# Graph convolution on one Trainium2 core: visits in two pieces, steps of four chunks in straight code, and a histogram that begins with the sources as they lie

## The chip, the core and the metric

The kernel runs on one core of one Trainium2 chip. The time is in device microseconds (us) from the start of one execution to its end; a kernel's time is the median of its runs. TensorE (PE in the profile) does the matmuls, VectorE (DVE) and ScalarE (ACT) the elementwise work, GpSimd (POOL) issues the gathers, and SyncE (SP) passes signals on and issues some of the transfers. PSUM is the accumulator memory of TensorE: eight banks of 128 x 512 fp32, called `bank` in the kernel.

## The reference

Two graph convolutions over the same graph, with a layer norm and a leaky ReLU between them, and a residual with a layer norm behind them:

```python
def _cheb_norm(src, dst, n):
    deg = jax.ops.segment_sum(jnp.ones((src.shape[0],), jnp.float32), src, num_segments=n)
    dinv = jnp.where(deg > 0, jax.lax.rsqrt(jnp.maximum(deg, 1.0)), 0.0)
    return -dinv[src] * dinv[dst]
...
    def prop(h):
        return jax.ops.segment_sum(h[src] * norm[:, None], dst, num_segments=x.shape[0])
    out = x @ W0
    tx1 = prop(x)
    out = out + tx1 @ W1
    return out + b
...
    h = _cheb_conv(x, src, dst, norm, W1_0, W1_1, b1)
    h = _layer_norm(h, gamma, beta)
    h = jnp.where(h >= 0, h, NEG_SLOPE * h)
    out = _cheb_conv(h, src, dst, norm, W2_0, W2_1, b2)
    return out
...
    x = _layernorm(x + _L0_gnn_ref(...), axis=-1)
```

`x` is 6250 x 512 in fp32. There are 106250 edges (50000 random ones in both directions, and one loop per node), sorted by `dst`. Each weight is 512 x 512.

## The kernel before

The nodes lie in 49 tiles of 128 rows (`TILES`), and `acc` holds all of them in SBUF: first `x`, then the sums of a pass. The kernel has four stages.

**Histogram.** The degrees are counted by matmul. In each of 24 visits DVE makes two one-hot arrays for 36 chunks of 128 sources each (`lo_hot`, 128 values, and `hi_hot`, 49 values; L805 and L808), and PE adds 36 products of them in one bank (L668). In the same visit PE turns one tile of `x` (L655, `turn`), ACT moves it to `feat` and SP stores it as `feat_dram[0]`. ACT also takes the squares of a tile and counts, with `Sign` activations, how many edges lie below each tile's end. Before the first visit all edge numbers are turned by PE and copied by DVE. After the visits the other 25 tiles are turned.

**Table.** Each tile, scaled by the node's factor (`up`), is split into a high and a low fp16 half (ACT L507, DVE L878) and stored as a row of 1024 fp16 in `table[0]`. Behind that DVE makes the small tables that tell each step its tile, group and ring slot (`neg_tile`, `tile_i`, `group_i`, `slot_i`, `used_i`), and `walk_ready` lets PE, SP and DVE begin the first pass.

**Two passes** (`l` = 0 and 1), one for each convolution. POOL gathers the 832 chunks of 128 edges by indirect DMA, 256 KB each, from `table[l]` into a ring of 16 chunk slots in SBUF (L444). A group is 2 chunks, so there are 416 groups and 8 ring slots of one group; POOL waits on `ring_free` before each group. A step is one pair of a group and a tile, since a group's edges can lie across the end of a tile: 416 + 48 = 464 steps. In a step DVE makes one one-hot array per chunk from `dst_c` (L923), PE multiplies them with the chunk's two halves, 4 matmuls into one of 4 banks (L710), and DVE adds the bank, times `down`, to the tile's rows of `acc` (L947). SP waits until a group has landed (L389) and tells PE (`groups_ready`), and in the same loop waits until the steps that used the group of 4 earlier (`FREE_LAG`) are done and tells POOL that its slot is free (`ring_free`, L393). SP also copies each block of 16 index columns from `src_u` to `index` by DMA (L371).

**Visits.** Once the sums of a tile are complete, a visit makes its output. Steps run in blocks of 8. After each block but every seventh comes a visit, whose place is fixed; a comparison of `early` with the tile's number skips it there if a tile could be late, and then all that are left come at the end of the pass. All 49 come in their places with these inputs. A visit on PE is one row of work in program order: the product of `base_in` and `wB` (L727), the turn of the sums (`staged`, L655), in the first pass the turns of two earlier tiles' normalized and hidden rows (L655), and then the product of the turned sums and `wA` (L749), for which PE waits until ACT has moved the turned sums from PSUM to `feat` (L564, `turned_moved`). In the first pass the output is normalized (statistics on DVE, L991), turned, scaled, put through the leaky ReLU, turned back and stored as `table[1]`. In the second it is added to `x`, normalized and stored as `out`.

The loops over blocks, periods, gathers and SP's turns are hardware loops (`looped`), with a few turns written out at either end.

## Time and profile before

| | us |
|---|---|
| median of 3 runs | 3432.88 (3428.44 to 3451.5) |
| span of the profiled execution | 3370.7 |
| the profiled execution's own time outside its span, taken as median less span | 62.2 |
| PE busy | 2065.1 (61%) |
| DVE busy | 1544.4 (46%) |
| ACT busy | 505.3 (15%) |
| POOL busy | 1700.9 (50%) |
| data of DMAs | 559.98 MB, mean 166 GB/s |

The span runs from the first to the last instruction in the trace. The time holds the start and the end of the execution too. No engine is busy over all of the span, so what counts is who waits for whom. A name such as "L444 POOL" is line 444 of the kernel on GpSimd. PEld is TensorE's loading of weights, which overlaps its matmuls; SPq, ACTq and DVEq are an engine's sequencer, as opposed to its data path.

### The profile page before, as it was taken

To read this page: it belongs to the slowest core of one execution; us is meant where nothing else is said; L and a number is where in the kernel's file an instruction comes from. 1 tells how busy PE (TensorE), PEld (TensorE's weight loads), DVE (VectorE), ACT (ScalarE), POOL (GpSimd) and SP (SyncE) were. 2 spreads that over 40 slices of the span, in tenths; PEclk is the share of its full clock that TensorE was granted. 3 is DMA by queue.
4 is the path that set the end of the run, shared out by engine and by line. 5 is a ranking of instruction groups with operands and counts; after the bars stand their busy time and mean duration, and the time that the engine had idled before them with its cause. 6 is when DMAs were issued, how large, how long until landed. Compare 5 with 4: busy or idle time off the path is not lost.

```text
span 3370.7 us, 41016 instructions
## 1 busy us (share of the span) xinstructions
PE 2065.1 (61%) x7250; PEld 963.6 (29%) x7251; DVE 1544.4 (46%) x3507; ACT 505.3 (15%) x1030; POOL 1700.9 (50%) x1725
## 2 busy tenths in 40 slices
PE   6836576665665665665764656565565656555655
PEld 5712232222222322232331222222222222222222
DVE  6754444444444444544443444444444434444444
ACT  5920111111111211111230000000000000000000
POOL 0156554545555554655526545554545445554543
PEclk6558887887887878887876878787777777878778
DMA  6376565655555555655646555565555555555554
GB/s 215 133 259 181 150 174 155 173 159 160 164 167 168 159 165 157 181 159 167 182 132 200 166 158 171 166 177 155 167 159 164 155 158 165 161 165 162 159 159 122
DMA packets 215109, 559.98 MB, mean 166 GB/s; under 512 B 48100, under 2 KB 49760, under 8 KB 214948
## 3 DMA queue, kind: packets, MB, share of 16 engines
q0 software_dynamic: 133120, 436.31, 45.9%
q10 hardware_dynamic: 44676, 81.73, 7.2%
q1 hardware_dynamic: 37152, 40.21, 3.6%
q8 instruction: 50, 0.82, 0.1%
q14 instruction: 111, 0.91, 0.1%
HBM read 493.08 MB, written 64.18 MB: 165 GB/s over the span
## 4 chain that ended last, share of the span: by engine, by line
PE 30%; another core or an unknown queue 26%; issue 25%; DVE 8%; ACT 5%; DVEq 3%; ACTq 1%; DMA 1%; POOL 1%; SPq 0%; POOLq 0%
PE bank L749 16%; PE bank L710 10%; DVE acc L947 6%; PE bank L668 2%; ACT work L556 2%; ACT feat L564 1%; DVEq L923 1%; PE bank L727 1%; PE bank L655 1%; DVEq L947 1%; DVE onehot L923 1%; POOL ring L444 1%; ACT work L546 1%; ACTq L528 0%
## 5 line engine op out<-in xcount | busy, mean ns | idle before, releaser
L444 POOL DMA_INDIRECT ring<-table,index x1664 | 1672.6, 1005 | 1466.5 <-SPq L393 952.1
L947 DVE SCALAR_TENSOR_TENSOR acc<-bank,down,acc 128x512 f32 x928 | 696.9, 751 | 1219.6 <-PE bank L710 709.8
L710 PE MATMUL bank<-ring,onehot 128*128 x3712 | 920.3, 406 | 306.0 <-issue 148.1
L749 PE MATMUL bank<-wA,feat 128*128 128x512 f32 x784 | 547.6, 863 | 804.2 <-ACT feat L564 748.2
L923 DVE TENSOR_SCALAR onehot<-count_h,dst_c,neg_tile 128x128 f16<-128x128 f16 x1856 | 489.2, 329 | 490.1 <-issue 487.6
L710 PEld LDWEIGHTS bank<-ring,onehot 128*128 128x128 f16 x3712 | 380.6, 103 | 865.6 <-issue 515.3
L749 PEld LDWEIGHTS bank<-wA,feat 128*128 128x128 f32 x784 | 212.0, 285 | 1084.9 <-ACT feat L564 774.3
L727 PE MATMUL bank<-wB,base_in 128*128 128x512 f32 x784 | 353.6, 594 | 0.0
L546 ACT ACTIVATE work<-acc 128x512 f32 (+1 forms) x98 | 61.7, 630 | 1747.4 <-issue 1039.3
L727 PEld LDWEIGHTS bank<-wB,base_in 128*128 128x128 f32 x784 | 149.5, 191 | 155.8 <-issue 142.1
L564 ACT ACTIVATE feat<-bank 128x512 f32<-128x512 f32 x98 | 58.5, 597 | 845.4 <-remote 828.7
L655 PE MATMUL bank<-ident,work 128*128 128x128 f32 x588 | 88.3, 288 | 125.8 <-issue 99.7
L655 PEld LDWEIGHTS bank<-ident,work 128*128 128x128 f32 x588 | 67.1, 145 | 199.1 <-issue 181.7
L668 PE MATMUL bank<-ring 128*128 128x49 bf16 x864 | 85.2, 275 | 2.5 <-DVE ring L808 2.5
L668 PEld LDWEIGHTS bank<-ring 128*128 128x128 bf16 x864 | 83.6, 146 | 4.0 <-DVE ring L808 2.9
L598 ACT ACTIVATE feat<-bank,beta_c,gamma_c 128x128 f32<-128x128 f32 x196 | 73.8, 457 | 59.2 <-remote 39.5
L556 ACT ACTIVATE work<-acc,shift,rstd 128x512 f32 (+1 forms) x98 | 78.4, 800 | 6.6 <-DVE shift L960 3.0
L991 DVE BATCH_NORM_STATS2 stats<-acc 128x6 f32 (+1 forms) x98 | 67.5, 689 | 11.7 <-issue 9.5
L655 PE MATMUL bank<-ident,acc 128*128 128x128 f32 x196 | 52.4, 425 | 27.4 <-ACT feat L480 18.6
L805 DVE TENSOR_TENSOR ring<-work,base_in 128x4608 bf16<-128x4608 bf16 x24 | 61.4, 2559 | 14.4 <-PE bank L668 14.2
L421 POOL PARTITION_ALL_REDUCE row_max<-row_max x1 | 0.4, 382 | 126.0 <-DVE row_max L821 126.0
L613 ACT ACTIVATE acc<-bank 128x512 f32 (+1 forms) x49 | 29.4, 600 | 141.9 <-PE bank L749 132.7
(118 smaller groups left out, 689.6 us busy)
## 6 DMA issues: line engine op xcount, KB each, us to landing
ring<-table,index POOLq DMA_INDIRECT x1664
base_in<-feat ACTq DMA_DIRECT2D x98, 256.0 KB
feat<-feat SPq DMA_DIRECT2D x49, 256.0 KB, 2.9
table<-work SPq DMA_DIRECT2D x49, 256.0 KB, 3.1
feat<-feat ACTq DMA_DIRECT2D x49, 256.0 KB
table<-work ACTq DMA_DIRECT2D x49, 256.0 KB
feat<-in_x ACTq DMA_DIRECT2D x48, 256.0 KB
out<-work ACTq DMA_DIRECT2D x48, 256.0 KB
```

The source lines that it names most:

```text
L444: nc.gpsimd.indirect_dma_start(out=ring[:, at * ROW:(at + 1) * ROW], out_offset=None, in_=table[l], in_offset=bass.IndirectOffsetOnAxis(ap ...
L546: nc.scalar.activation(staged[it.slot % 2], tile_of(acc, it.n), ACT.Copy).then_inc(staged_ready, 1)
L556: nc.scalar.activation(normed[s], tile_of(acc, k.n), ACT.Identity, bias=shift[:, k.slot % 3:k.slot % 3 + 1], scale=rstd[:, k.slot % 3:k.sl ...
L564: nc.scalar.activation(feat[:, 2 + s, :], bank[TURN_BANK][:, :], ACT.Copy).then_inc(turned_moved, 1)
L598: last = nc.scalar.activation(feat[:, s, c * P:(c + 1) * P], bank[NORMED_BANK][:, c * P:(c + 1) * P], ACT.Identity, bias=beta_c[:, c:c + 1 ...
L655: last = nc.tensor.transpose(to[:, c * P:(c + 1) * P], src_tile[:, c * P:(c + 1) * P], ident[:, :])
L668: last = nc.tensor.matmul(bank[4][:, 0:TILES], lo_hot[it.slot % 2][:, :, j], hi_hot[it.slot % 2][:, :, j], start=it.least == 0 and j == 0, ...
L710: last = nc.tensor.matmul(bank[u % SUM_BANKS][:, :], onehot[:, u, j, :], ring[:, bass.ds(at, D)], start=j + half == 0, stop=j + half == GROUP)
L727: nc.tensor.matmul(to[:, :], base_in[:, tile_slot, c * P:(c + 1) * P], wB[:, c * D:(c + 1) * D], start=c == 0, stop=False)
L749: last = nc.tensor.matmul(to[:, :], feat[:, 2 + tile_slot, c * P:(c + 1) * P], wA[:, c * D:(c + 1) * D], start=False, stop=c == KB - 1)
L923: last = nc.vector.tensor_scalar(onehot[:, slot, j, :], count_h[:, :], col(dst_c, group * GROUP + j), col(neg_tile, n), ALU.subtract, ALU. ...
L947: nc.vector.scalar_tensor_tensor(tile_of(acc, tile[u]), bank[u % SUM_BANKS][:, :], col(down[:, l, :], tile[u]), tile_of(acc, tile[u]), ALU ...
```

## The change

Group and step: a group is 4 chunks, a pass has 208 groups and 208 + 48 = 256 steps of 8 matmuls. The ring keeps its 16 chunk slots, now 4 groups, and `FREE_LAG` is 2. DVE makes the one-hot arrays of two steps in one instruction, from `rel` (for each step and chunk, the edges' places relative to the step's tile) and a row of counts in PSUM; it adds a step's bank to `acc` without a factor, and the factor `down` comes in where the sums are turned, by a product with the diagonal matrix `diag`.

Visits: a visit has two pieces on PE, `begin` (the turn of the tile before, the product with `wB`, the turn of the sums) and `complete` (the product with `wA` and the turn of the hidden rows), two steps apart (`PRODUCT_LATER`). ACT's move of the turned sums lies between them. Visits come 5.2 steps apart. DVE's part comes 1 and 3 steps after `begin`.

Loops: the passes are written out, with no hardware loops on any engine. The gathers take their indices from a whole table in SBUF, so SP's index DMAs are gone, and they have no bounds check.

Histogram: 26 visits of 32 chunks, with 4 sources of a node value side by side in the one-hot arrays. It begins with the sources of the first 128 groups as they lie, one group to a partition, since a count doesn't depend on where an edge lies; the turn into columns for the gathers comes behind the first visit. Counts 0 to 255 and the identity are made on DVE, and the count of groups below each tile's end is made by DVE and two small matmuls in place of ACT's `Sign`. From the third visit on PE turns two tiles of `x` in each. The tables for the steps are made behind the table stage (`tables`, `relative`), and the lateness of visits, the bias parts and the second pass's factors behind the first one-hot arrays.

```diff
     LAST_ROWS = N - (TILES - 1) * P
     BOUNDS = TILES - 1
-    GROUP = 2
-    GROUPS = -(-E // (GROUP * P))
+    GROUP = 4
...
     CHUNKS = GROUPS * GROUP
     STEPS = GROUPS + BOUNDS
-    UNROLL = 8
-    STEP_BLOCKS = STEPS // UNROLL
-    GATHER_BLOCKS = GROUPS // UNROLL
-    RING = UNROLL
-    FREE_LAG = 4
...
+    RING = 16 // GROUP
+    FREE_LAG = RING // 2
...
     SUM_BANKS = 4
-    HIST_VISITS = BOUNDS // 2
-    HIST = 36
...
+    HIST = 32
+    RUN = 4
+    HIST_VISITS = CHUNKS // HIST
...
-    LAG_STATS, LAG_NORMAL, LAG_HIDDEN, LAG_LEAKY, LAG_BACK, LAG_LOW = 1, 2, 3, 4, 5, 6
...
+    SPACING = STEPS * 256 // TILES
+    FIRST_PLACE = -(-STEPS // TILES) + 8 // GROUP
+    PRODUCT_LATER, LEAKY_LATER, STATS_LATER = 2, 1, 3
...
-                def pass_on(it, l=l):
...
-                    for k in range(UNROLL):
-
-                        sp.wait_ge(ring_landed[k], 16 * GROUP * (GATHER_BLOCKS * l + it.n + 1))
-                        sp.sem_inc(groups_ready, 1)
-                        if k >= first:
-
-                            sp.wait_ge(steps_done, used[k - first] + STEPS * l)
-                            sp.sem_inc(ring_free, 1)
...
+                for g in range(GROUPS):
+                    k = g % RING
...
+                    sp.wait_ge(ring_landed[k], 16 * GROUP * ((GROUPS * l + g) // RING + 1))
+                    sp.sem_inc(groups_ready[l], 1)
+                    if g >= FREE_LAG:
+
+                        sp.wait_ge(steps_done[l], used[g - FREE_LAG - first])
+                        sp.sem_inc(ring_free, 1)
...
-                def gathers(it, l=l):
-                    pool.wait_ge(index_in[it.slot], 16 * (GATHER_BLOCKS // 2 * l + it.turn + 1))
-                    pool.sem_inc(gathers_begun, 1)
...
-                        wait(pool, ring_free, GROUPS * l + it.n * UNROLL + k - RING + 1)
...
-                        for j in range(GROUP):
...
-                            nc.gpsimd.indirect_dma_start(
-                                out=ring[:, at * ROW:(at + 1) * ROW], out_offset=None, in_=table[l],
-                                in_offset=bass.IndirectOffsetOnAxis(ap=index[:, it.slot, at:at + 1], axis=0),
-                                bounds_check=bound, oob_is_err=False).then_inc(ring_landed[k], 16)
-
-                straight(gathers, 0, 2, 2)
-                looped(pool, gathers, 2, GATHER_BLOCKS, 2)
...
+                for g in range(GROUPS):
...
+                    wait(pool, ring_free, GROUPS * l + g - RING + 1)
+                    for j in range(GROUP):
+                        at = k * GROUP + j
+                        c = index_col(g * GROUP + j)
+                        nc.gpsimd.indirect_dma_start(
+                            out=ring[:, at * ROW:(at + 1) * ROW], out_offset=None, in_=table[l],
+                            in_offset=bass.IndirectOffsetOnAxis(ap=index[:, c:c + 1].bitcast(U32), axis=0)
+                        ).then_inc(ring_landed[k], 16)
...
+            for v in range(HIST_VISITS):
+                pe.wait_ge(hot_ready, v + 1)
+                for j in range(HIST):
+                    last = nc.tensor.matmul(bank[4][:, 0:TILES], lo_hot[v % 2][:, j // RUN, :, j % RUN],
+                                            hi_hot[v % 2][:, j // RUN, :, j % RUN],
+                                            start=v == 0 and j == 0, stop=v == HIST_VISITS - 1 and j == HIST - 1,
+                                            skip_group_check=True)
+                last.then_inc(hist_done, 1)
...
+                for k in range(max(2 * (v - TURN_LATER), 0), max(2 * (v - TURN_LATER) + 2, 0)):
+                    turn_x(k)
...
+            def step(l, n, need, slot_at):
+                g = STEPS * l + n
+                for j in range(GROUP):
...
+                            if n % BLOCK == 0:
+                                pe.wait_ge(onehots_ready, g // BLOCK + 1)
+                            if n == 0:
+                                wait(pe, sums_added, g - SUM_BANKS + 1)
+                            pe.wait_ge(groups_ready[l], need & NEED)
+                        if j == GROUP - 1 and half == 1 and n + 1 < STEPS:
...
+                            wait(pe, sums_added, g + 1 - SUM_BANKS + 1)
+                        last = nc.tensor.matmul(bank[n % SUM_BANKS][:, :], hot,
+                                                ring[:, bass.ds(slot_at + (2 * j + half) * D, D)],
+                                                start=j + half == 0, stop=j + half == GROUP)
+                last.then_inc(steps_done[l], 1)
...
+            def turn_sums(l, v, steps):
+
+                pe.wait_ge(sums_added, STEPS * l + steps)
...
+                for c in range(KB):
+                    last = nc.tensor.matmul(bank[TURN_BANK][:, c * P:(c + 1) * P],
+                                            acc[:, bass.ds(v * D + c * P, P)], diag[:, v % 2, :],
+                                            start=True, stop=True)
+                last.then_inc(sums_turned, 1)
+
+            def sums_product(l, v):
+
+                pe.wait_ge(sums_moved, TILES * l + v + 1)
+                dense(out_bank(numbered(v)), sums_t[v % 2], wA, False).then_inc(out_done, 1)
...
+            def begin(l, v, steps):
+                if l == 0 and v > 0:
+                    turn_normed(v)
+                base_product(l, v)
+                turn_sums(l, v, steps)
+
+            def complete(l, v):
+                sums_product(l, v)
+                if l == 0 and v > 0:
+                    turn_hidden(v)
...
-                        pe.wait_ge(staged_ready, TILES * l + it.n + 1)
-                        wait(pe, turned_moved, TILES * l + it.n)
-                        turn(staged[tile_slot], bank[TURN_BANK], sums_turned)
...
-                        nc.tensor.matmul(to[:, :], ones_b[0:BIAS_PARTS, :], bias_parts[:, l * D:(l + 1) * D],
-                                         start=False, stop=False)
-                        pe.wait_ge(turned_moved, TILES * l + it.n + 1)
-                        for c in range(KB):
-                            last = nc.tensor.matmul(to[:, :], feat[:, 2 + tile_slot, c * P:(c + 1) * P],
-                                                    wA[:, c * D:(c + 1) * D], start=False, stop=c == KB - 1)
-                        last.then_inc(out_done, 1)
...
-                walk(pe, early, steps, visit)
...
+                for n in range(STEPS):
...
+                    step(l, n, entry[2 * (n % LOADED)], entry[2 * (n % LOADED) + 1])
+                    for v in range(BOUNDS):
+                        if place(v) == n + 1:
+                            with pe.If(early > v):
+                                begin(l, v, n + 1)
+                        if due(v, PRODUCT_LATER) == n + 1:
+                            with pe.If(early > v):
+                                complete(l, v)
...
+            dve.wait_ge(s_src[0], 16)
+            low_high(0, P * GROUP, edge_in[0][:, 0, :])
...
+            def sources(v):
+                wait(dve, hist_done, v - 1)
...
+                nc.vector.tensor_tensor(lo_hot[v % 2], lo_want.unsqueeze(1).to_broadcast([P, runs, P, RUN]),
+                                        columns(src_lo, P), ALU.is_equal)
+                nc.vector.tensor_tensor(hi_hot[v % 2], hi_want.unsqueeze(1).to_broadcast([P, runs, TILES, RUN]),
+                                        columns(src_hi, TILES), ALU.is_equal).then_inc(hot_ready, 1)
...
+            for k in range(TILES):
+                low_rows(k)
+            tables()
+            relative()
             dve.sem_inc(walk_ready, 1)
...
+            def hots(l, b):
...
+                nc.vector.tensor_tensor(onehot[:, b % 2, :, :], count_p.unsqueeze(1).to_broadcast([P, HOTS, P]),
+                                        rel[:, b * HOTS:(b + 1) * HOTS].unsqueeze(2).to_broadcast([P, HOTS, P]),
+                                        ALU.is_equal).then_inc(onehots_ready, 1)
...
-                def hot(n, tile, slot):
...
-                    for j in range(GROUP):
-                        last = nc.vector.tensor_scalar(onehot[:, slot, j, :], count_h[:, :],
-                                                       col(dst_c, group * GROUP + j), col(neg_tile, n),
-                                                       ALU.subtract, ALU.is_equal)
-                    last.then_inc(onehots_ready, 1)
...
-                def steps(b, least, l=l):
...
-                        dve.wait_ge(steps_done, STEPS * l + n + 1)
-
-                        wait(dve, sums_added, STEPS * l + n)
-                        nc.vector.scalar_tensor_tensor(tile_of(acc, tile[u]), bank[u % SUM_BANKS][:, :],
-                                                       col(down[:, l, :], tile[u]), tile_of(acc, tile[u]),
-                                                       ALU.mult, ALU.add).then_inc(sums_added, 1)
...
+                    dve.wait_ge(steps_done[l], n + 1)
+                    wait(dve, sums_added, g)
+                    nc.vector.tensor_tensor(acc_at, acc_at, bank[n % SUM_BANKS][:, :], ALU.add).then_inc(sums_added, 1)
+                    if n % BLOCK == BLOCK - 1:
+                        hots(l, n // BLOCK + 2)
```

TensorE in the first pass, a visit between two blocks of steps, before:

```order
L287 COMPARE_AND_BRANCH
L727 MATMUL bank<-wB,base_in 128x512 x4
L655 MATMUL bank<-ident,work 128x128 x8
L655 MATMUL bank<-ident,feat 128x128 x4
L745 MATMUL bank<-bias_parts,ones_b 128x512
L749 MATMUL bank<-wA,feat 128x512 x4
L287 UNCONDITIONAL_BRANCH
L698 TENSOR_LOAD group_i
L698 TENSOR_LOAD slot_i
```

and now, the first piece, with the step behind it:

```order
L795 COMPARE_AND_BRANCH
L638 MATMUL bank<-ident,work 128x128 x4
L708 MATMUL bank<-wB,base_in 128x512 x4
L741 MATMUL bank<-bias_parts,ones_b 128x512
L752 MATMUL bank<-diag,acc 128x128 x4
L795 UNCONDITIONAL_BRANCH
L697 REGISTER_ALU
L701 ISA
L701 MATMUL bank<-ring,onehot 128x512
```

and two steps on, the second piece:

```order
L701 ISA
L701 MATMUL bank<-ring,onehot 128x512
L798 COMPARE_AND_BRANCH
L708 MATMUL bank<-wA,work 128x512 x4
L638 MATMUL bank<-ident,feat 128x128 x4
L798 UNCONDITIONAL_BRANCH
```

The turn of the sums, now a product with `diag`, and the product with `wA`, which stood in one row, have two steps of 8 matmuls (L701) between them. The turn of the normalized rows has moved ahead of the product with `wB`, and that of the hidden rows behind the product with `wA`.

VectorE in a pass, where it goes over from the adds of one block to the one-hot arrays of the next, before:

```order
L947 ISA
L947 SCALAR_TENSOR_TENSOR acc<-bank,down,acc 128x512
L947 ISA
L947 SCALAR_TENSOR_TENSOR acc<-bank,down,acc 128x512
L929 TENSOR_LOAD tile_i
L923 ISA
L923 TENSOR_SCALAR onehot<-count_h,dst_c,neg_tile 128x128
L923 ISA
L923 TENSOR_SCALAR onehot<-count_h,dst_c,neg_tile 128x128
```

and now, at any place between visits:

```order
L1029 TENSOR_TENSOR onehot<-bank,rel 128x1024
L1128 TENSOR_LOAD tile_i
L1134 ISA
L1134 TENSOR_TENSOR acc<-acc,bank 128x512
L1134 ISA
L1134 TENSOR_TENSOR acc<-acc,bank 128x512
L1029 TENSOR_TENSOR onehot<-bank,rel 128x1024
L1134 ISA
L1134 TENSOR_TENSOR acc<-acc,bank 128x512
```

What came in blocks of 16 one-hot arrays and 8 adds is now one wide one-hot instruction behind every second add, and 2 adds stand between two one-hot instructions.

## Rows read from the trace of the kernel before

**Rows 1.** The page: span, then costliest groups (xcount, busy us, mean ns, idle time before).

```profile
span 3370.7 us, 41016 instructions
...
L444 POOL DMA_INDIRECT ring<-table,index x1664 | 1672.6, 1005 | 1466.5 <-SPq L393 952.1
...
L947 DVE SCALAR_TENSOR_TENSOR acc<-bank,down,acc 128x512 f32 x928 | 696.9, 751 | 1219.6 <-PE bank L710 709.8
...
L710 PE MATMUL bank<-ring,onehot 128*128 x3712 | 920.3, 406 | 306.0 <-issue 148.1
...
L923 DVE TENSOR_SCALAR onehot<-count_h,dst_c,neg_tile 128x128 f16<-128x128 f16 x1856 | 489.2, 329 | 490.1 <-issue 487.6
```

**Rows 2.** Waits, whole span: engine and line, releaser, us in total, times, longest us.

```profile
POOL ring L444 <- SPq L393: 952.1, 182, 11.6
...
ACT feat L564 <- remote: 828.7, 91, 13.3
...
PE bank L749 <- ACT feat L564: 748.2, 83, 13.0
```

**Rows 3.** Timeline, second pass, one visit with gathers under way (start us, us, engine, line).

```profile
2636.36 1.04 PE L655 MATMUL bank<-ident,work 128*128 128x128 f32 x4 [2.64 <-issue]
...
2642.09 1.00 POOL L444 DMA_INDIRECT ring<-table,index  x1 [0.30 <-issue]
...
2645.26 0.60 ACT L564 ACTIVATE feat<-bank 128x512 f32<-128x512 f32 x1 [8.32 <-remote]
...
2645.91 5.78 PE L749 MATMUL bank<-wA,feat 128*128 128x512 f32 x8 [7.97 <-ACT feat L564]
...
2651.53 7.07 PE L710 MATMUL bank<-ring,onehot 128*128 x32
...
2653.40 1.00 POOL L444 DMA_INDIRECT ring<-table,index  x1 [10.31 <-SPq L393]
```

**Rows 4.** Timeline, end of the first pass: a visit after the last gather.

```profile
1725.68 1.00 POOL L444 DMA_INDIRECT ring<-table,index  x1 [0.30 <-issue]
...
1744.95 0.60 ACT L564 ACTIVATE feat<-bank 128x512 f32<-128x512 f32 x1 [0.72 <-PE bank L655]
...
1774.87 1.00 POOL L444 DMA_INDIRECT ring<-table,index  x1 [48.19 <-issue]
```

**Rows 5.** Busy time by stretch: us and, in brackets, instructions of each engine, granted clock, DMA.

```profile
1786.00:1798.00 12.00, 7.10 (x22) 2.15 (x20) 3.00 (x4) 0.00 (x0) 9.26 (x10) 0.78 0.71 198
...
1802.00:1814.00 12.00, 0.00 (x0) 0.00 (x0) 0.75 (x1) 0.00 (x0) 9.00 (x9) 0.50 0.70 200
...
201.30:1712.00 1510.70, 948.80 (x3149) 423.53 (x3150) 689.00 (x1646) 238.24 (x494) 828.44 (x821) 0.81 0.58 167
...
1775.00:3335.00 1560.00, 925.85 (x2824) 390.55 (x2824) 668.31 (x1601) 99.25 (x187) 832.71 (x832) 0.78 0.57 165
```

**Rows 6.** Timeline, the stage ahead of the first gather.

```profile
134.72 1.05 PE L655 MATMUL bank<-ident,acc 128*128 128x128 f32 x4
...
135.56 3.55 PE L668 MATMUL bank<-ring 128*128 128x49 bf16 x36
...
139.15 0.21 DVE L817 TENSOR_SCALAR deg<-bank 128x49 f32<-128x49 f32 x1 [4.75 <-PE bank L668]
...
46.53 2.56 DVE L805 TENSOR_TENSOR ring<-work,base_in 128x4608 bf16<-128x4608 bf16 x1 [0.67 <-PE bank L668]
...
201.28 1.69 POOL L444 DMA_INDIRECT ring<-table,index  x1 [6.16 <-issue]
...
L878 DVE SCALAR_TENSOR_TENSOR work<-acc,up,work 128x512 f16<-128x512 f16 (+1 forms) x49 | 34.4, 745 | 11.2 <-ACT work L507 11.2
```

**Rows 7.** Timeline, last gather and last store.

```profile
3333.24 1.00 POOL L444 DMA_INDIRECT ring<-table,index  x1 [0.30 <-issue]
...
3363.73 0.27 ACTq L587 DMA_DIRECT2D out<-work  x1
```

**Rows 8.** The page: a queue that fetches instructions (packets, MB, share of 16 engines).

```profile
q14 instruction: 111, 0.91, 0.1%
```

1165 lines of the change are left out of this document (634 added, 531 removed).

## Prediction

> **What bounds the kernel now.** I read the page's costliest groups first, then the waits, then the timeline of one cycle of the ring, then the same work with no gathers under way, then busy time by stretch.
>
> The groups say that no engine is full: POOL issues 1664 gathers at 1.005 us each and is idle as long again, 952.1 us of it waiting for SP to free a ring slot [rows 1, 2]. The second large pair of waits is one chain: ACT waits 828.7 us for something marked "remote" before it moves the turned sums (L564), and PE waits 748.2 us for that move before the product with wA (L749) [rows 2].
>
> The timeline shows how the two belong together. In the second pass PE ends the turn of a tile's sums at 2637.40 (2636.36 + 1.04), and ACT, whose only need is that turn's signal, starts at 2645.26, after 8.32 us of waiting. What happened between is that POOL started the last of 16 gathers at 2642.09; about 3.2 us after it ACT moves. Then comes the product, 5.78 us, and then 32 matmuls of steps in 7.07 us, 0.221 each, and with their first steps the next gather at 2653.40, after 10.31 us idle [rows 3]. At the end of the first pass, where the last gather started at 1725.68 and the next one comes only 48.19 us later, the same L564 follows PE's turn in 0.72 us [rows 4]. So the signal is late while gathers stream and prompt when they don't. Two stretches of the same pass say it of all engines: at the same DMA rate (198 and 200 GB/s) and 10 and 9 gathers, PE ran 22 matmuls in one and none in the other, and DVE 4 instructions and 1 [rows 5]. Bandwidth is therefore not the bound. The kernel runs in cycles: POOL fills 16 slots in 16 x 1.305 = 20.9 us (1.005 and the gap of 0.30) and in the later part of it the signals of the other engines stop arriving; the ring fills, POOL stops, the signals come through, PE works off its queue, and slots come free. 1664 / 16 = 104 such cycles would be the least; 182 waits add to 952.1 us, 9.15 us per 16 gathers.
>
> **Ahead of the first gather.** Before, the histogram ends at 139.15; the 36 matmuls of a visit take 3.55 us, 98.6 ns each, and one turn of x 1.05 [rows 6]. Now PE is the likely pace: 832 matmuls x 0.0986 = 82.0, 49 turns x 1.05 = 51.5, and some 8 for the small turns and products, 142 us. It can start once the first sources have landed and been split, which I put at 12 us, an estimate (one load and four small DVE operations stand ahead, in place of all loads, turns and copies of the edges), so it ends at about 154, 15 later. From 139.15 to the first gather at 201.28 it was 62.1 us: 49 DVE operations of the table stage at 0.745 are 36.5, their waiting for ACT 11.2, and 14.4 are left for the factor ahead and the small tables behind [rows 6]. Now the moves of x no longer trail into the table stage (2 of waiting in place of 11.2), and the largest row norm is taken during the histogram (9.1 in place of 14.4): 154 + 36.5 + 2 + 9.1 = 201.6, **0 us**. Bounds: DVE's wide one-hot array took 2.56 and, by its width, the narrow one 1.0 [rows 6], 3.6 for 36 chunks; 32 chunks at that rate are 3.2 and hide under PE's 5.4 per visit; if the layout with 4 sources side by side ran at half the rate, 12 + 26 x 6.4 = 178 would be the end, +24. If PE ran at double clock there, 15 could be gained.
>
> **Steps.** PE's matmuls rise from 3712 to 4096, since each of the 96 pairs that cross a tile's end costs 8 matmuls instead of 4: 384 x 0.221 to 384 x 0.406 = 85 to 156 us of PE [rows 1, 3]. They aren't all on the path: PE is busy 925.85 of the 1560 us of a pass [rows 5]. They lie mostly in the time when PE works off its queue, though, so I carry them in the cost of a cycle below. DVE's 1856 one-hot instructions (489.2 us) become 256 wide ones, and 928 adds (696.9) become 512; at 0.751 an add that is 384 us [rows 1]. What a wide one takes no row shows; between 8 x 0.1 (no fixed part) and 8 x 0.329 = 2.6 us it is at most 674 us in all. DVE was not waited for, so I count **0**, with its order as a bound: an add behind a wide one-hot can be 2.6 us late, and PE has 4 banks of slack against that.
>
> **The visit.** The wait of PE for ACT's move gets two steps in front of the product. What it hides depends on the size of the wait: 748.2 / 98 = 7.6 us a visit, of which 16 matmuls at 0.256 (nearer to 0.221 than to the mean of 0.406, since they run off a queue) cover 4.1 if their chunks have landed. 3.5 remain. By PE's own account a visit with its steps then takes 20.6 busy (19.1 before, by 1874.65 us in both passes over 98, plus 3.9 matmuls and the slower turn), 3.5 of waiting and the 4.6 of other idle time that it has now: 28.7, against 31.3 now (3070.7 over 98). That is -258 over the passes.
>
> **The pauses**, from POOL's side. The slots and their bytes are the same, so are the cycles, 104. What follows a filled ring is now: landing and release 2.2 (from the last gather's end at 2643.09 to ACT's start, [rows 3]), then, where PE had stopped within the steps, one step of 8 matmuls and its signals, 2.6: 4.8 us. Where it had stopped at a product, 2.2 + 0.6 for the move + 5.78 for the product + a step of 2.6 = 11.2. Before, the second kind was the rule, since 98 visits' waits take most of 104 cycles: 83 waits of PE at L749 [rows 2]. With two steps between the pieces I take one cycle in four: 0.75 x 4.8 + 0.25 x 11.2 = 6.4. 104 x 6.4 = 666 against 952: **-286**. The two accounts agree to 10%, and I take this one, since POOL's chain has no gaps in it.
>
> **Between the passes and behind the last gather.** The first pass's last gather starts at 1725.68 and the second's first 48.19 us after its end [rows 4]; in it lie steps, and then visits' pieces with lags of up to 6 visits that have to be drained one by one (LAG_LOW). Now the lags are one tile, so of some five drained rows two are left: 31, **-18**. From the last gather at 3333.24 to the last store at 3363.73 and the end at 3370.7 it is 37.5 [rows 7]; with its product and normalization alone behind the last step, 25, **-12**.
>
> **Loops, bounds checks and index DMAs.** POOL's cadence of 1.305 was the same in every row, at loop ends too; without the bounds check it could fall, by at most the 0.30 of the gap: 0 to -0.3 x 1664 = -499, but only where the ring has a slot free. As the ring empties at PE's pace I take **0**. The Trainium skill, page "Runtime: NRT & Kernel Launch", section "Instruction fetch mechanics", says that a taken branch breaks the sequential prefetch and costs a fetch by DMA, and that unrolled code is preferred for that. By that rule the late signals could be late instructions, fetched behind the gathers' packets. The larger of the two queues that fetch instructions moved 111 packets in the whole execution, 0.1% of the span [rows 8], for some 100 turns of hardware loops: the rows neither exclude it nor speak for it. It is the rival "full flow" below.
>
> **The sum**, against the profiled execution: 3370.7 + 0 - 286 - 18 - 12 = 3054.7; with the 62.2 outside the span, which is the median's remainder, **3117 us**.
>
> **Rivals.**
>
> *Full flow.* The late signals come of the loops or of the sheer number of instructions and signals, and straight code with half of them doesn't have it. For it: streaming alone doesn't stop the signals, for they still come through 11 to 23 us after the second pass's first gather [rows 4, 5]. Against it: in the cycle shown ACT moves as soon as the last gather is out [rows 3], and a late instruction of ACT would not end just there. It would give up to 3054.7 + 286 - 952.1 = 2389 of span, 2451 with the rest, and PE would then be nearly full (20.6 us busy of the 22.2 that 1664 / 98 = 17 gathers at 1.305 take), which I price at 100: about 2550.
>
> *Little gained.* The signals stay as late, and PE now stops at the product in half of the cycles, since two steps ahead of it also need chunks that haven't been passed on: 0.5 x 4.8 + 0.5 x 11.2 = 8.0, x 104 = 832, -120 in place of -286: 3283. For it: landed chunks are announced by SP, whose signals are late as well.
>
> *Slower.* Freed slots come in fours of chunks, and with a lag of 2 groups POOL waits, in each cycle, for a whole step and a piece of a visit: 11.2 every time, 1165 us, +213 against now, so 3433 + 213 - 30 = 3616. It decides from a pause of 9.4 us on (952.1 and the 30 of the other terms, over 104). For it: a group of 4 needs 4 landings and 8 matmuls before it frees anything, at 0.406 each where the clock is low [rows 1]. Against it: two groups, 8 chunks, can always be on the way meanwhile.
>
> *Late visits* (a tile that misses its place puts all others behind the pass) would cost over 98 x 5 us; by the graph's own counts each tile has its last group two steps or more ahead of its place. 1 in 100.
>
> **How the numbers follow.** Forecast with its own range 2950 to 3260: 0.52. Full flow 0.22, little gained 0.15, slower 0.09, late visits 0.01, no effect at all 0.01. About 1% is what a measurement of this kernel can tell from no change. Within 1% (3399 to 3467) falls part of the way from little gained to slower: 0.06; above it 0.09; faster 0.85. The range goes from the full flow's 2540 to 3400, which leaves out the slower cases and the lowest part of full flow.
>
> **What would show it.** In the new profile: POOL's wait for SP at the gathers, 666 us in about 104 waits, each near 5 or 11; ACT's wait for PE's turn still marked "remote" and 7 us or more; PE's wait at the product with wA halved; the first gather near 201; between the passes 31. If POOL's wait is below 300 us and ACT's move follows PE's turn in under 1 us with gathers under way, full flow was right and my reading of the signals' cause was wrong. If the first gather comes after 215, the one-hot layout is slow. The forecast fails most likely through its one argued number, the share of cycles in which PE stops at a product.

## The result, and the profile after

The changed kernel takes **2681.27 us** (2671.0 to 2690.22, 4 runs) against 3436.52 for the kernel before: a ratio of 0.780, 95% interval 0.7775 to 0.7834. I had forecast 3117 with a range of 2540 to 3400, so the time lies in the range, but the gain is 755 us and not 316. The profiled execution has a span of 2688.4 us and a time of its own of 2690.22.

The page, as in [rows 1]: the span, the gathers, the steps' matmuls, DVE's adds, its one-hot arrays, and the product with wA, which L708 shares with that of wB.

```profile
span 2688.4 us, 28747 instructions
...
L397 POOL DMA_INDIRECT ring<-table,index x1664 | 1575.8, 947 | 940.6 <-issue 467.0
L701 PE MATMUL bank<-ring,onehot 128*128 x4096 | 1012.7, 403 | 177.1 <-SPq L361 87.1
L1134 DVE TENSOR_TENSOR acc<-acc,bank 128x512 f32 x512 | 351.3, 686 | 1622.7 <-remote 881.3
...
L708 PE MATMUL bank<-wA,work 128*128 128x512 f32 x784 | 429.0, 698 | 174.3 <-ACT work L496 148.5
...
L1029 DVE TENSOR_TENSOR onehot<-bank,rel 128x1024 f16<-128x1024 f32 x256 | 311.6, 1218 | 0.1
```

A gather takes 0.947 in place of 1.005, and it waits 467.0 us for nothing but the 0.30 between two. The adds fell from 696.9 to 351.3 us, the one-hot arrays from 489.2 to 311.6, at 1.218 each. PE's busy time is what it was (2063.3 against 2065.1), at a granted clock of 0.878 in place of 0.780.

The waits, as in [rows 2]:

```profile
DVE acc L1134 <- remote: 881.3, 112, 14.2
ACT work L496 <- remote: 616.5, 53, 62.3
...
POOL ring L397 <- SPq L365: 433.2, 163, 4.8
...
PE bank L708 <- ACT work L496: 148.5, 36, 7.0
```

POOL waits 433.2 us for a free slot where it waited 952.1, in 163 waits of at most 4.8. PE's wait for ACT's move of the sums fell from 748.2 to 148.5. The waits marked remote are still there: ACT's is 616.5 where it was 828.7, and DVE now has 881.3 where it had 268.0. "Remote" is the profile's word for a signal that comes long after the instruction that gives it had ended.

The timeline of the second pass, one cycle of the ring, as in [rows 3]:

```profile
2009.06 1.16 PE L752 MATMUL bank<-diag,acc 128*128 128x128 f32 x8
...
2010.06 3.84 PE L701 MATMUL bank<-ring,onehot 128*128 x16
...
2014.32 0.60 ACT L496 ACTIVATE work<-bank 128x512 f32<-128x512 f32 x1 [8.10 <-remote]
...
2014.97 3.70 PE L708 MATMUL bank<-wA,work 128*128 128x512 f32 x8 [1.08 <-issue]
...
2015.98 0.95 POOL L397 DMA_INDIRECT ring<-table,index  x1 [0.30 <-issue]
...
2018.51 1.89 PE L701 MATMUL bank<-ring,onehot 128*128 x8
...
2019.44 0.69 DVE L1134 TENSOR_TENSOR acc<-acc,bank 128x512 f32 x1 [11.74 <-remote]
2019.62 0.94 POOL L397 DMA_INDIRECT ring<-table,index  x1 [2.69 <-SPq L365]
```

PE ends the turn of the sums at 2010.22, and ACT's move comes at 2014.32, after a wait of 8.10 marked remote: the signal comes 4.1 us late. But PE has gone on with 16 matmuls of steps, and runs the product at 2014.97 while gathers still stream. Here the late signal came with gathers under way, 1.7 us before the last gather of the burst; that is the rarer case. Of the 177 waits marked remote of more than 1 us between the first and the last gather, 141 end while POOL stands still, the median 2.5 us after the end of the last gather, and 36 while it streams. The last gather of the burst starts at 2015.98 and ends at 2016.93. DVE, 11.74 us without a signal, adds at 2019.44, and POOL starts again at 2019.62 after 2.69 us. Before, it was 10.31 [rows 3]: there the steps that free a slot had yet to be run when the signals came through, and here they had been run.

Whose signals are late can be read more closely than I did. Every wait marked remote in these traces, but for waits of POOL and PE of at most 1.4 us, is one of ACT or DVE for something that PE gives: the turned sums, turned rows, a step done. What DVE and ACT give is prompt, with gathers under way too. Here, in the second pass, a burst begins at 2588.15, and 12 us into it ACT starts 0.04 us after the end of the DVE instruction that it waits for (2600.04 + 0.18):

```profile
2588.15 0.94 POOL L397 DMA_INDIRECT ring<-table,index  x1 [2.98 <-SPq L365]
...
2600.04 0.18 DVE L1068 BATCH_NORM_AGGREGATE mean_var<-stats 128x2 f32<-128x6 f32 x1
2600.26 0.29 ACT L501 ACTIVATE std<-mean_var,eps 128x1 f32<-128x1 f32 x1 [11.58 <-DVE mean_var L1068]
```

All 97 waits of ACT on that line end 0.04 us after DVE, and PE's product comes 0.05 us after ACT's move in 96 of 96 waits before the change. So it is TensorE's signals that are held. Since the profile models the ends of matmuls, it can't tell a late signal from a matmul that ends late.

The gathers that bound each stage, and the histogram, as in [rows 4, 6, 7]; first the histogram's one-hot arrays and matmuls late in that stage, then its end, the first gather, the last of the first pass, the first of the second, and the last:

```profile
98.75 2.28 DVE L888 TENSOR_TENSOR ring<-work,base_in 128x4096 bf16<-128x4096 bf16 x1
...
98.89 1.75 PE L652 MATMUL bank<-ring 128*128 128x49 bf16 x32 [0.53 <-DVE ring L890]
...
103.84 0.21 DVE L999 TENSOR_SCALAR deg<-bank 128x49 f32<-128x49 f32 x1 [0.19 <-PE bank L652]
...
143.50 1.10 POOL L397 DMA_INDIRECT ring<-table,index  x1 [2.97 <-DMA table<-work]
...
1396.18 0.95 POOL L397 DMA_INDIRECT ring<-table,index  x1 [0.30 <-issue]
...
1434.57 0.94 POOL L397 DMA_INDIRECT ring<-table,index  x1 [37.45 <-DMA table<-work]
...
2656.05 0.95 POOL L397 DMA_INDIRECT ring<-table,index  x1 [0.30 <-issue]
```

From them the two spans divide as follows. The pauses are what is left of the time from first to last gather, without the piece between the passes, when 1662 intervals of the undisturbed cadence are taken off.

| | before, us | after, us | difference |
|---|---|---|---|
| start to first gather | 201.3 | 143.5 | -57.8 |
| 1662 intervals at 1.306 and 1.251 | 2170.6 | 2079.2 | -91.4 |
| pauses in the two passes | 912.2 | 395.0 | -517.2 |
| last gather of one pass to first of the next | 49.2 | 38.4 | -10.8 |
| last gather to the end | 37.4 | 32.3 | -5.1 |
| span | 3370.7 | 2688.4 | -682.3 |

The medians differ by 755, since the profiled execution of the kernel before was 64 us shorter than its median (taking 1.8 us outside the span, as after) and that of the kernel after 9 us longer.

### The profile page after: what moved, and what is told of

The parts are those of the page before. It is cut to its first block, busy times and chain, and to the rows that moved or that the text cites. A ratio compares the mean times of both kernels' runs of the same rounds, so it can differ in the third digit from the quotient of the medians.

```text
span 2688.4 us, 28747 instructions
## 1 busy us (share of the span) xinstructions
PE 2063.3 (77%) x8006; PEld 979.2 (36%) x8006; DVE 978.1 (36%) x1503; ACT 415.2 (15%) x844; POOL 1609.5 (60%) x1721
## 3 DMA queue, kind: packets, MB, share of 16 engines
q0 software_dynamic: 133120, 436.31, 54.9%
## 4 chain that ended last, share of the span: by engine, by line
another core or an unknown queue 33%; PE 29%; issue 18%; DVE 10%; ACT 5%; ACTq 2%; DMA 2%; DVEq 0%; POOL 0%; SPq 0%
PE bank L701 13%; PE bank L708 12%; DVE acc L1134 2%; PE bank L752 2%; DMA feat<-feat 2%; DVE onehot L1029 1%; ACT work L507 1%; ACT feat L517 1%; ACT work L496 1%; DVE work L1010 1%; DVE stats L1065 1%; PE bank L638 1%; DVE ring L888 1%; ACT std L501 1%
## 5 line engine op out<-in xcount | busy, mean ns | idle before, releaser
L397 POOL DMA_INDIRECT ring<-table,index x1664 | 1575.8, 947 | 940.6 <-issue 467.0
L701 PE MATMUL bank<-ring,onehot 128*128 x4096 | 1012.7, 403 | 177.1 <-SPq L361 87.1
L1134 DVE TENSOR_TENSOR acc<-acc,bank 128x512 f32 x512 | 351.3, 686 | 1622.7 <-remote 881.3
L701 PEld LDWEIGHTS bank<-ring,onehot 128*128 128x128 f16 x4096 | 420.8, 103 | 719.8 <-issue 340.4
L708 PE MATMUL bank<-wA,work 128*128 128x512 f32 x784 | 429.0, 698 | 174.3 <-ACT work L496 148.5
L708 PE MATMUL bank<-wB,base_in 128*128 128x512 f32 x784 | 378.9, 629 | 13.4 <-DVE acc L1100 8.1
L708 PEld LDWEIGHTS bank<-wA,work 128*128 128x128 f32 x784 | 171.8, 226 | 389.8 <-issue 215.2
L1029 DVE TENSOR_TENSOR onehot<-bank,rel 128x1024 f16<-128x1024 f32 x256 | 311.6, 1218 | 0.1
L752 PE MATMUL bank<-diag,acc 128*128 128x128 f32 x784 | 134.2, 323 | 144.3 <-DVE acc L1134 67.7
L708 PEld LDWEIGHTS bank<-wB,base_in 128*128 128x128 f32 x784 | 156.4, 205 | 180.5 <-issue 165.2
L496 ACT ACTIVATE work<-bank 128x512 f32<-128x512 f32 x98 | 58.5, 597 | 883.3 <-remote 616.5
L752 PEld LDWEIGHTS bank<-diag,acc 128*128 128x128 f32 x784 | 113.1, 222 | 168.7 <-DVE acc L1134 106.4
L888 DVE TENSOR_TENSOR ring<-work,base_in 128x4096 bf16<-128x4096 bf16 x26 | 59.4, 2286 | 9.3 <-PE bank L652 8.9
L652 PE MATMUL bank<-ring 128*128 128x49 bf16 x832 | 45.6, 230 | 13.8 <-DVE ring L890 13.8
```

The costliest lines, as they stand in the source:

```text
L397: nc.gpsimd.indirect_dma_start(out=ring[:, at * ROW:(at + 1) * ROW], out_offset=None, in_=table[l], in_offset=bass.IndirectOffsetOnAxis(ap ...
L496: nc.scalar.activation(sums_t[k % 2], bank[TURN_BANK][:, :], ACT.Copy).then_inc(sums_moved, 1)
L652: last = nc.tensor.matmul(bank[4][:, 0:TILES], lo_hot[v % 2][:, j // RUN, :, j % RUN], hi_hot[v % 2][:, j // RUN, :, j % RUN], start=v == ...
L701: last = nc.tensor.matmul(bank[n % SUM_BANKS][:, :], hot, ring[:, bass.ds(slot_at + (2 * j + half) * D, D)], start=j + half == 0, stop=j + ...
L708: last = nc.tensor.matmul(to[:, :], x_of[:, c * P:(c + 1) * P], w[:, c * D:(c + 1) * D], start=start and c == 0, stop=not start and c == K ...
L752: last = nc.tensor.matmul(bank[TURN_BANK][:, c * P:(c + 1) * P], acc[:, bass.ds(v * D + c * P, P)], diag[:, v % 2, :], start=True, stop=True)
```

## The experiments

One thing came out at once and has to stand first. **The kernel before does not always take 3436 us.** The runs below were taken in six sets, each on one chip and with the kernel before beside them. In three sets it took 2442 to 2446, in the other three 3381 to 3451; one chip was in both groups, at different times. Where it takes 2442, no kernel shows a wait marked remote of any size and POOL's pauses come to under 40 us in all (the rests of e12 apart); I call these sets *flowing*, the others *held*. All of the tables above are of held executions. Runs are compared within a set unless another is named: the kernel after itself was timed beside the result and in the set of e5 and e6 only.

The data of the gathers are not slower where signals are held: the packets of queue q0, which carries them, took 54.9% of a span of 2688.4 us in the kernel after and 63.7% of 2308.8 in e5, 1476 and 1471 us. What makes one set held and another flowing no run shows.

| run | kernel | in this set before took | it took |
|---|---|---|---|
| e1 | after, product in one row with the turn | 2442 | 2307 |
| e2 | before, groups of 4 | 2442 | 2463 |
| e3 | before, straight code, no index DMAs | 2442 | 2441 |
| e4 | after, gathers of 1 KB rows | 2442 | 2292 |
| e5 | after | 2446 | 2311 (ratio 0.9445, 0.943 to 0.946) |
| e6 | after, bounds check back | 2446 | 2384 |
| e7 | after, RUN = 8 | 3451 | 2719 |
| e8 | as e1 | 3451 | 3240 |
| e9 | as e2 | 3451 | 2954 |
| e10 | as e3 | 2442 | 2443 |
| e11 | after, product 3 steps later | 2442 | 2323 |
| e12 | after, rests of 2.1 us | 2442 | 2728 |
| e13 | as e3 | 3442 | 3377 |
| e14 | as e11 | 3442 | 2676 |
| e15 | as e12 | 3442 | 2725 |
| e16 | after, rests of 0.5 us | 3381 | 2660 |
| e17 | after, rests of 1.1 us | 3381 | 2651 |
| e18 | after, 2.1 us behind 16 gathers | 3381 | 2687 |

e1, e2, e5 and e6 were run 4 times each and e3 10 times; of the others there is one run each, and a difference of some 2% between held runs of one kernel is not to be read.

**Two pieces, one row (e1, e8).**

```diff
                 turn_sums(l, v, steps)
+                sums_product(l, v)
 
             def complete(l, v):
-                sums_product(l, v)
```

> The kernel after the change, with the product of the turned sums and wA put back behind the turn of the sums, in one row, as before the change; the turn of the hidden rows stays two steps on. Three theories. Pieces (mine): signals between engines are still held while gathers stream, and what was won is that TensorE has two steps to run while it waits for ScalarE's move. Then POOL's pauses go back to 9 or 10 us each, about 104 of them, 990 us in place of 395, and the time to 3200 to 3300. Straight code: the gain comes of the loops being gone; then this stays within 60 us of 2681. Larger steps: the gain comes of 4 chunks to a signal; then TensorE still waits at the product but catches up sooner, 2800 to 2950.

> The first experiment again. Where the kernel before takes 2440 us on this chip, 2307 again, and no signal held. Where it takes 3430, signals are held, and the three theories part: pieces 3200 to 3300, larger steps 2800 to 2950, straight code within 60 us of 2681.

Flowing, it took 2307 against the 2311 of e5, a ratio to the kernel before of 0.944 in both: the second piece is worth nothing there. Held, it took 3240, as expected of the pieces (3200 to 3300) and 559 over the 2681 of the kernel after. Its waits are near those of the kernel before (engine and line, releaser, us, times, longest):

```profile
POOL ring L397 <- SPq L365: 954.8, 160, 14.3
ACT work L496 <- remote: 709.7, 50, 62.3
```

954.8 for the 952.1 of before, 709.7 for 828.7. 83 of POOL's pauses are more than 5 us over the cadence, as many as before. The timeline of one of its cycles in the second pass:

```profile
2206.27 0.94 POOL L397 DMA_INDIRECT ring<-table,index  x1 [10.80 <-SPq L365]
...
2220.72 2.08 PE L752 MATMUL bank<-diag,acc 128*128 128x128 f32 x8 [4.11 <-issue]
...
2225.90 0.95 POOL L397 DMA_INDIRECT ring<-table,index  x1 [0.30 <-issue]
2229.18 0.60 ACT L496 ACTIVATE work<-bank 128x512 f32<-128x512 f32 x1 [15.47 <-remote]
...
2229.83 5.21 PE L708 MATMUL bank<-wA,work 128*128 128x512 f32 x8 [7.03 <-ACT work L496]
...
2237.08 0.95 POOL L397 DMA_INDIRECT ring<-table,index  x1 [10.23 <-SPq L365]
```

The burst of gathers starts at 2206.27, the turn of the sums comes 14.5 us into it, ACT hears of it at 2229.18, 2.3 us after the last gather's end (2225.90 + 0.95), and then the product, 5.21 us, stands between POOL and its next slot: 10.23 us of rest.

**Groups and steps of four chunks (e2, e9).**

```diff
-    GROUP = 2
+    GROUP = 4
...
-    UNROLL = 8
+    UNROLL = 4
...
-    FREE_LAG = 4
+    FREE_LAG = 2
...
-    FIRST_PLACE = 2
+    FIRST_PLACE = 8
```

> The kernel before the change with groups and steps of 4 chunks: blocks of 4 steps, a ring of 4 groups, a free lag of 2, the first visit behind block 9, all else as it was (hardware loops, index DMAs, one-piece visits). Pieces: TensorE is stopped at the product in nearly every cycle of the ring whatever a step's size, so the time stays within 80 us of 3433. Larger steps: a pause has one signal's delay less and TensorE gets further ahead of DVE: 3000 to 3200. Straight code: no change but the 384 matmuls more, 3450 to 3550.

> The second experiment again. Where the kernel before takes 2440 us, 2463 again. Where it takes 3430: pieces within 80 us of 3433, larger steps 3000 to 3200, straight code 3450 to 3550.

Flowing, it is 0.8% slower (ratio 1.008, 1.006 to 1.010). Held, it takes 2954, 497 less than the kernel before, and POOL's wait is down to 545.2 in the old one-piece visits. None of the expectations had this: by the account of the pieces, mine, it was to stay within 80 us of 3433, and by that of larger steps to take 3000 to 3200.

```profile
POOL ring L444 <- SPq L393: 545.2, 134, 12.0
...
ACT feat L564 <- remote: 274.0, 36, 16.2
```

The timeline of a visit in its second pass:

```profile
2204.82 0.99 POOL L444 DMA_INDIRECT ring<-table,index  x1 [2.85 <-SPq L393]
...
2207.96 3.60 PE L727 MATMUL bank<-wB,base_in 128*128 128x512 f32 x8
...
2211.40 0.60 PE L655 MATMUL bank<-ident,work 128*128 128x128 f32 x4
...
2212.03 0.60 ACT L564 ACTIVATE feat<-bank 128x512 f32<-128x512 f32 x1 [1.51 <-issue]
...
2212.68 3.70 PE L749 MATMUL bank<-wA,feat 128*128 128x512 f32 x8 [0.37 <-issue]
```

Here the gathers start again at 2204.82, and the visit comes at once behind, the turn of the sums 6.6 us into the burst; ACT's move follows in no time (2212.03). So both parts of the change act on the same pauses, and they don't simply add: groups of 4 alone on the kernel before give 497, and taking the second piece out of the kernel after loses 559, of 755 in all. The second piece alone on the kernel before wasn't run, so no share can be put to each. Why groups of 4 do well with one-piece visits in the kernel before and badly in the kernel after is read off these two timelines only: a visit every 4 steps falls into the first 10 us of a burst in the one, and one every 5.2 steps into its later part in the other. No run tested that alone; it is open.

**Straight code (e3, e10, e13).** `looped` calls `straight`, the gathers read `src_u`, and `stage_index` is gone.

```diff
-    with eng.Fori(0, (z - a) // slots) as i:
-        for slot in range(slots):
-            visit(Item(a + i * slots + slot, slot, a // slots + i, a + slot, slots))
+    straight(visit, a, z, slots)
```

> The kernel before the change with every hardware loop written out and the gathers' indices read straight from the table in SBUF, so that SP's index DMAs are gone; groups of 2, one-piece visits and bounds checks as they were. Straight code: most of the gain, 2700 to 2950. Pieces and larger steps: the held signals stay, POOL's wait for SP stays at 850 to 950 us; the time is 3433 less at most 60 at the loops' ends, 3370 to 3440.

> The third experiment again. Where the kernel before takes 2440 us on this chip, 2441 again. Where it takes 3440, signals are held: if straight code and the missing index DMAs had a share in the gain, 100 us or more less; if not, 3380 to 3450, and POOL's pauses stay at 850 to 950.

> As for the run before of this kernel. Where the kernel before takes 3440: if straight code and the missing index DMAs had a share in the gain, 100 us or more less; if not, 3380 to 3450 with POOL's pauses at 850 to 950. Where it takes 2440: 2441.

Flowing 2441 and 2443 for 2442, a ratio of 0.9997 (0.999 to 1.001). Held 3377 for 3442, 65 less, which held runs of the kernel before also lie apart (3381 to 3451), with POOL's wait unchanged:

```profile
POOL ring L436 <- SPq L389: 955.3, 153, 11.8
ACT feat L556 <- remote: 878.6, 88, 14.6
```

Loops, their branches and the index DMAs had no share that can be seen, in the flow or in the holds.

**The kernel after where nothing is held, and the bounds check (e5, e6).** e6 puts `bounds_check=bound, oob_is_err=False` back.

> The kernel after the change, unaltered, on whatever chip this is. On a chip where the kernel before takes 2442 us (as in the first experiments) no signals are held, POOL's own cadence is the bound, and the time should be 144 ahead of the first gather, 1664 x 1.25 for the gathers, and 70 between and behind the passes: 2294, within 20. On a chip where the kernel before takes 3430 it should be 2680 again.

> The kernel after the change with the bounds check back at each gather. If the check sets a gather's time on POOL (1.005 us before, 0.947 after), each gather is 0.055 us longer and the time 90 us longer than that of the kernel after the change on a chip where POOL is the bound; if the shorter gather came of the index's place in SBUF or of the code without loops, it stays within 15.

The page's group of the gathers, e5:

```profile
L397 POOL DMA_INDIRECT ring<-table,index x1664 | 1584.6, 952 | 551.8 <-issue 496.5
```

and e6:

```profile
L398 POOL DMA_INDIRECT ring<-table,index x1664 | 1667.7, 1002 | 538.0 <-issue 503.4
```

e5 took 2311, and but for the piece between the passes and 25.7 us of short waits for SP, POOL waits for nothing but the 0.30 us: the gathers are the bound. A gather takes 0.952 without and 1.002 with the check, 83 us over 1664 of them. The time is 73 us more (2384), and the span of the profiled execution 68, since POOL's short waits for SP fall from 25.7 to 5.7. The shorter gather is the missing check, all of it.

What the change gives in the flow can be read off the spans of e5 and of e3, whose kernel takes the flowing time of the kernel before: 2308.8 and 2437.8, 129 less. The first gather comes at 145.2 in place of 200.4, 55 us, and 1662 intervals of 1.254 in place of 1.303 are 81. What is left is between the passes 12 less, in small pauses 14 more, and behind the last gather 5 more. So in the flow the gain is the histogram's and the missing check's, and pieces and larger groups give nothing.

**The histogram's layout (e7).** `RUN = 8` in place of 4.

> The kernel after the change with 8 sources of a node value side by side in the histogram's one-hot arrays instead of 4 (RUN = 8). A matmul of the histogram took 98.6 ns where a weight column's elements lie 36 apart, and 55 where they lie 4 apart, at the same pace whether the granted clock was 0.5 or 1.0. If it is that distance, 8 apart gives between 55 and 99 ns; if the new layout's other features did it (32 in place of 36, the shorter one-hot array), 55. DVE's wide one-hot array stays at 2.29 us.

The page's group of the histogram's matmuls in e7:

```profile
L652 PE MATMUL bank<-ring 128*128 128x49 bf16 x832 | 83.7, 276 | 6.6 <-DVE ring L890 6.6
```

and in the kernel after:

```profile
L652 PE MATMUL bank<-ring 128*128 128x49 bf16 x832 | 45.6, 230 | 13.8 <-DVE ring L890 13.8
```

83.7 / 832 = 101 ns a matmul against 45.6 / 832 = 55; the kernel before had 98.6 [rows 6]. The first gather comes at 179.5 instead of 143.5, and that is 36 of the 58 us won ahead of it. With elements 8 apart (16 bytes) a matmul is as slow as with 36 apart, with 4 apart (8 bytes) it is fast. Both one-hot arrays have the same distance in each kernel, so no run tells whether it is the loading of the weights (`lo_hot`) or the reading of the 49 columns (`hi_hot`) that pays for it. The clock doesn't do it. Here are 40 us of the histogram in the kernel before, and then in e3, by stretch (the columns of [rows 5]):

```profile
60.00:100.00 40.00, 40.00 (x385) 39.56 (x384) 34.04 (x20) 37.10 (x87) 0.00 (x0) 0.50 0.55 194
```

```profile
60.00:100.00 40.00, 40.00 (x385) 39.57 (x383) 33.93 (x20) 37.03 (x87) 0.00 (x0) 1.00 0.55 188
```

385 matmuls, turns among them, in 40 us at a granted clock of 0.50 and 385 at 1.00: 99 ns for each of the histogram's in both (85.2 and 85.4 us for 864).

**A third step between the pieces (e11, e14).** `PRODUCT_LATER, LEAKY_LATER, STATS_LATER = 3, 1, 4`.

> The kernel after the change with the second piece of a visit 3 steps behind the first instead of 2 (DVE's statistics at 4 instead of 3). If TensorE still stops at the product in some cycles while signals are held, a third step helps there: 2560 to 2650 where the kernel after takes 2681. If two steps were enough and it is DVE's and SP's held signals that stop it, no change. Where no signals are held: 2311, no change.

> As for the run before of this kernel. Where the kernel before takes 3440: 2560 to 2650 if TensorE still stops at the product in some cycles, 2680 if it is DVE's and SP's held signals that stop it. Where it takes 2440: 2320.

2323 flowing and 2676 held, no gain in either (POOL's wait 401.1 for 433.2). PE's wait for ACT's move at the product, 148.5 us in the kernel after, is 2.8 in e14, and the time is the same: the waits that two steps leave cost nothing.

**Rests for POOL (e12, e15 to e18).** Behind every eighth gather POOL writes zeros to a spare buffer, four times; each write waits for the one before.

```diff
+                    if g % 2 == 1:
+                        for _ in range(4):
+                            wait(pool, paced, paces[0])
+                            nc.gpsimd.memset(spare[:, :], 0.0).then_inc(paced, 1)
+                            paces[0] += 1
```

> The kernel after the change, with POOL writing zeros to a spare buffer four times behind every eighth gather, some 2.5 us in which no gather starts. If a hold sets in after some 10 us of gathers in a row and ends when POOL rests for about 2 us, the bursts are now too short for it: ScalarE's and DVE's waits marked remote all but vanish, POOL's waits for SP fall from 433 us to under 100, and the time is 208 x 2.5 = 520 over the 2294 of undisturbed gathers, 2780 to 2850. If the hold doesn't depend on the bursts' length, the waits for SP stay and the 520 come on top: 2950 to 3200. Where no signals are held: 2780 to 2830.

> As for the run before of this kernel, which took 2728 undisturbed. Where the kernel before takes 3440: 2728 to 2800, with POOL's waits for SP under 100 us and hardly a wait marked remote, if a hold needs a long burst of gathers; 2900 to 3150 with the waits as they were if it doesn't.

2728 flowing and 2725 held: the same time where the kernel before lies 1000 us apart. (Both are less than expected, since a rest came out at 2.13 us and not 2.5.) This is the run on which the explanation rests. It was held, as its waits show, where e12 has no wait marked remote. The waits of e15:

```profile
POOL ring L400 <- issue: 475.6, 1662, 0.3
...
DVE acc L1142 <- remote: 200.7, 57, 9.9
...
ACT work L504 <- remote: 83.1, 14, 6.7
```

There is no wait for SP in the list, and the waits marked remote fell from 881.3 to 200.7 on DVE and from 616.5 to 83.1 on ACT. They haven't vanished, as I had expected them to, but nothing is late for them. Of the 73 that are over 1 us, 70 end while POOL rests, the median 1.85 us after the end of the last gather: the held signals come through in the rest.

> One write of zeros behind every eighth gather, a rest of 0.53 us. Where the kernel before takes 2440: 2294 + 208 x 0.53 = 2405 to 2425. Where it takes 3440: if any rest breaks a burst, the same, 2405 to 2450; if a rest must be about 2 us for the held signals to come through, as the last gather's end and the release lie 2.2 apart, the waits for SP come back: 2650 to 2750.

> Two writes, a rest of 1.07 us behind every eighth gather. Where the kernel before takes 2440: 2515 to 2535. Where it takes 3440: the same, 2515 to 2550, if 1 us is enough, 2650 to 2750 if not.

> Four writes behind every sixteenth gather, 2.13 us. Where the kernel before takes 2440: 2515 to 2535. Where it takes 3440: 16 gathers take 20 us, more than the 10 to 14 after which a hold sets in, so signals are held in the second half of each burst; with two steps of work ahead TensorE bridges it in part: 2580 to 2680.

With 0.53 and 1.07 us behind 8 gathers the waits are back (DVE's remote 868.0 and 849.3), and so with 2.13 behind 16 (835.2). Of the rests tried, only 2.13 us behind every 8 gathers kept POOL from waiting. It isn't all or nothing: POOL's wait for SP, 433.2 without rests, is 310.5, 172.8 and 189.6 in e16, e17 and e18, so the rests take the place of pauses in part. And e17 and e18, which fall short alike, have the same mean pace of gathers, while that of e15 is slower; that it is the pace that counts, and not the length of a rest and of a burst, wasn't tested. The times, 2660, 2651 and 2687, are within 1.2% of the 2681 of the kernel after, which wasn't run in that set; none is a clear gain.

**Half the bytes (e4)** was to tell bytes from descriptors as the cause of the holds. Each gather takes 1 KB rows of other data, and the steps multiply the first half of a chunk twice.

> The kernel after the change, but each gather takes 128 rows of 1 KB instead of 2 KB (the table seen as rows of half the width, so other data), and the steps multiply the first half of a chunk twice; as many gathers, matmuls and signals. If the signals are held by the bytes of the gathers, ScalarE's wait marked remote before the move of the sums and DVE's before its adds fall by more than half and the passes run near 1.25 us a gather, 2350 to 2450. If they are held by the making of descriptors, which is the same, waits and time stay, 2600 to 2690.

It fell on a flowing set, where there is nothing to explain, and took 2292, as POOL's cadence says (1.251). What in the gathers holds the signals stays open.

## Why the prediction was right and wrong

**The bound and its mechanism: right in the main.** Signals are held in the later part of a burst of gathers, and most come through some 2 to 2.5 us after its last gather. e15 shows it. But I had written of the signals "of the other engines", and they are TensorE's alone. What I had not seen either, and could not from one trace, is that this is a condition of the execution and not of the kernel: the same program flows at other times.

**The pauses, -286: the right sign, the wrong size; measured -517.** The step that failed is "then, where PE had stopped within the steps, one step of 8 matmuls and its signals, 2.6", together with "one cycle in four" at the product. The runs show some 170 pauses in place of 104, with a median of 2.4 us over the cadence, and but for the one between the passes none is over 4.5; 2.3 us on average, where I had 6.4. PE does still stop at the product, 36 times and for 148.5 us in all, as here (first pass):

```profile
407.13 0.94 POOL L397 DMA_INDIRECT ring<-table,index  x1 [0.30 <-issue]
...
410.80 0.94 POOL L397 DMA_INDIRECT ring<-table,index  x1 [2.73 <-SPq L365]
...
411.09 6.12 PE L708 MATMUL bank<-wA,work 128*128 128x512 f32 x8 [5.38 <-ACT work L496]
```

POOL's next gather starts before the product does, since the slot was freed by a step that PE had run ahead of it. So it is with all 34 of these stops that are over 1 us: none of their products starts in a pause. Before the change 79 of 81 did, and in e8 48 of 49. Nor is a step's time in most pauses: in 118 of the 165 over 1 us no step of PE ended in the 0.7 us ahead of the next gather, and the pause is the release alone; in 47 one did. I had priced PE as if it stood still until it heard, in a kernel whose change was that it needn't. The other account, by PE's work and waits, had the same fault, and that the two agreed to 10% proved nothing: both took the product's waits over from the kernel before. That the time still fell inside the range is owed to the range, which reached down to another rival's 2540.

**The bounds check, 0: wrong; measured -91.** I had written that it counts "only where the ring has a slot free". By my own picture of a cycle, 16 gathers and then a pause, each gather lies on the path in full. The term was 1664 times the difference of 0.055 between two gathers' starts, and that lay inside my bounds of 0 and 0.3.

**Ahead of the first gather, 0 (-15 to +24): wrong; measured -58.** The histogram ended at 103.8, not 154. The step that failed is 832 x 0.0986: in the new layout it is 832 x 0.055 (e7), worth 36. And the bound of -15 was a slip: DVE's 3.2 a visit from 12 us on give 95, which was the lower end of the stage, 44 sooner than before. DVE did set the pace, 2.28 + 0.96 a visit. The table stage was shorter too, 39.7 from 103.8 to the gather in place of the 47.6 worked out: its 49 DVE operations took 32.6 without a wait, and the small tables run beside the landing of the last rows.

**Between and behind: -18 and -12, measured -10.8 and -5.1.** Right in sign, about half in size.

**The 62.2 us outside the span: wrong.** It is 1.8 us in the kernel after (2690.22 against 2688.4). The time of the profiled execution of the kernel before isn't known; if it is the same there, the other 60 were its distance from the median, and held runs of this kernel lie that far apart.

**The rivals.** *Full flow* named an end state that exists, for the wrong reason: the flowing executions are it, at 2311, and there the kernel before flows too. It was priced too high, since the gathers come earlier and are shorter than I had them, and PE, priced at 100 us, costs next to nothing there. By the rule of the Trainium skill, page "Runtime: NRT & Kernel Launch", section "Instruction fetch mechanics", a taken branch whose target isn't in the part of the code at hand costs a fetch, which straight code avoids; here e3, e10 and e13 show no gain from it, and the fetch queues moved 146 packets in the kernel after for 161 before. *Little gained* and *slower* did not occur; e8 shows that what *slower* feared, a stop at the product within the pause (10.23 us in the cycle shown), was real in this kernel without the second piece, and the second piece is what removed it.

## What to carry to other kernels

Where a releaser is unknown or remote and its wait ends when another engine pauses, price the pause by what is still undone when it opens, not by the whole chain behind it: work that needs no news during the wait is worth more than a shorter wait. If a time rests on such a wait, run the kernel before again at another time before explaining it; here more than a quarter of the kernel's time was a condition of the execution, and where it is absent the change is worth 5.5% and not 22%. And in a model of bursts and pauses, every instruction of the burst is on the path.

## What the runs showed that I had not expected

- The same program took 2442 and 3381 to 3451 us at different times, once on the same chip. In the slower executions TensorE's signals come late during long bursts of gathers 1.25 to 1.31 us apart, while those of VectorE and ScalarE stay prompt and the gathers' data are as fast. With 2.1 us without a gather behind every 8 POOL no longer waits, at 2725 held and 2728 flowing; 1.07 us isn't enough, nor are 2.1 behind 16.
- With bf16 elements 16 or 72 bytes apart in both operands in SBUF, a matmul of 128x128 weights and 49 columns took 101 and 99 ns, 8 bytes apart 55 ns, and the 99 ns came at a granted clock of 0.50 and of 1.00 alike.
- The bounds check of an indirect DMA costs 0.05 us of POOL a gather (1.002 against 0.952).
